# First attention of a two-layer block: the row scale takes the mask flag as an operand per partition, and moves with the mask maximum behind a second value copy

## The reference

```python
def _L0_xattn_ref(hidden_states, memory_tokens, memory_mask):   # hidden = layernorm(x), tokens (4, 1601, 256)
    scale = 1.0 / jnp.sqrt(jnp.asarray(D, hidden_states.dtype))
    scores = jnp.einsum('bsd,bmd->bsm', hidden_states, memory_tokens) * scale
    scores = jnp.where(memory_mask[:, None, :], scores, neg_inf)
    attn = jax.nn.softmax(scores, axis=-1)
    readout = jnp.einsum('bsm,bmd->bsd', attn, memory_tokens)
    valid_b = jnp.any(memory_mask, axis=-1)
    out = jnp.where(valid_b[:, None, None], readout, jnp.zeros_like(readout))
    return out
...
x = x + _L0_xattn_ref(_layernorm(x, axis=-1), ctx_2048, mask_BxS2_bk0)
```

## Time and profile before

| | |
|---|---|
| median of 3 runs | 760.24 us (758.79 to 761.08) |
| the profiled execution's own time | 762.05 us |
| its span in the profile | 759.1 us |
| busy over the span: PE / DVE / ACT / POOL | 92% / 72% / 52% / 23% |
| mean granted clock of PE | 0.97 of full speed |
| chain that ended last: PE / ACT / DVE / DMA | 64% / 11% / 10% / 3% |
| in it, `valid` L1571 and `rscale` L1626 | 1% each |

### The profile page before, as it was taken

How to read it: one execution, slowest core, us unless ns; L and a number is a source line. 1 busy time by engine, 2 the same in 40 slices (tenths; PEclk the granted TensorE clock), 3 DMA queues, 4 the chain that set the end, 5 groups by cost and what they waited for, 6 DMA issues and landing times.

```text
span 759.1 us, 14907 instructions
## 1 busy us (share of the span) xinstructions
PE 695.1 (92%) x5499; PEld 538.5 (71%) x5499; DVE 544.3 (72%) x1174; ACT 397.7 (52%) x564; POOL 173.8 (23%) x220
## 2 busy tenths in 40 slices
PE   3798999989889999999999699999999999998990
PEld 3798999988678888888888554454454454677880
DVE  6767576777486666666666788789888878766655
ACT  2643333334322322222222699999999999533550
POOL 5462524340000000000000050002303604442551
PEclk9899999999999999999999899999999999799996
DMA  7456484832627777677768959986969740464545
GB/s 247 133 172 227 134 293 146 266 125 89 201 65 242 231 255 239 209 224 243 253 217 170 149 81 168 189 128 95 221 92 201 119 67 2 151 253 130 165 129 190
DMA packets 55211, 131.14 MB, mean 173 GB/s; under 512 B 10112, under 2 KB 36096, under 8 KB 51568
## 3 DMA queue, kind: packets, MB, share of 16 engines
q1 hardware_dynamic: 51888, 122.93, 60.8%
q0 software_dynamic: 2256, 6.18, 2.4%
q10 hardware_dynamic: 1008, 1.25, 0.5%
HBM read 78.78 MB, written 48.79 MB: 168 GB/s over the span
## 4 chain that ended last, share of the span: by engine, by line
PE 64%; issue 11%; ACT 11%; DVE 10%; DMA 3%; SPq 1%; POOL 0%; DVEq 0%; POOLq 0%; ACTq 0%
PE ps L657 15%; PE ps L658 14%; PE ps L659 14%; ACT p L1439 8%; PE ps L1001 5%; PE ps L1189 4%; PE ps L959 3%; PE ps L1205 2%; PE ps L1023 1%; PE ps L741 1%; DVE valid L1571 1%; DVE rscale L1626 1%; PE ps L1173 1%; DMA raw<-in_ctxT 1%; ACT hh L1344 1%
## 5 line engine op out<-in xcount | busy, mean ns | idle before, releaser
L1439 ACT ACTIVATE p<-ps,kbias 128x1024 f32<-128x1024 f32 (+1 forms) x208 | 211.4, 1163 | 5.1 <-PE ps L959 4.9
L1950 DVE TENSOR_SCALAR p<-p 128x1024 f32<-128x1024 f32 (+1 forms) x208 | 140.8, 689 | 25.8 <-ACT p L1439 24.1
L1001 PE MATMUL ps<-p,vsl 128*17 128x256 f32 (+1 forms) x1664 | 114.2, 383 | 2.0 <-DVE p L1950 1.0
L959 PEld LDWEIGHTS ps<-qst,kst 48*128 48x128 f32 (+1 forms) x832 | 58.6, 182 | 60.0 <-ACT p L1439 32.1
L1344 ACT ACTIVATE hh<-h 128x512 fp32r<-128x512 f32 x50 | 31.6, 632 | 132.2 <-DVE h L1817 115.2
L959 PE MATMUL ps<-qst,kst 48*128 48x256 f32 (+1 forms) x832 | 91.1, 318 | 5.3 <-ACT p L1439 1.5
L360 POOL TENSOR_SCALAR nv<-mv 128x2 f32<-128x2 f32 x8 | 6.2, 777 | 358.8 <-DVE mv L1880 211.2
L657 PE MATMUL ps<-xTh,w_hi 128*128 128x512 f32 x200 | 79.8, 399 | 1.5 <-DVE h L1813 0.8
L658 PE MATMUL ps<-xTl,w_hi 128*128 128x512 f32 x200 | 79.2, 396 | 0.0
L659 PE MATMUL ps<-xTh,w_lo 128*128 128x512 f32 x200 | 78.9, 394 | 0.0
L1001 PEld LDWEIGHTS ps<-p,vsl 128*17 128x17 f32 (+1 forms) x1664 | 35.7, 96 | 40.0 <-DVE p L1950 7.2
(11 more groups left out here) (308 smaller groups left out, 1558.8 us busy)
## 6 DMA issues: line engine op xcount, KB each, us to landing
x_slots<-blank SPq DMA_DIRECT2D x20, 1032.0 KB, 5.9
kst<-k_hi SPq DMA_DIRECT2D x64, 200.2 KB, 8.4
w_raw<-in_w SPq DMA_DIRECT2D x25, 384.0 KB, 3.5
v_one<-vst SPq DMA_DIRECT2D x4, 1768.0 KB, 9.9
vsl<-v_one SPq DMA_DIRECT2D x4, 1768.0 KB, 17.0
kst<-k_lo SPq DMA_DIRECT2D x32, 200.2 KB, 8.5
raw<-in_ctxN SPq DMA_DIRECT2D x12, 512.0 KB, 5.6
e_w<-in_w SPq DMA_DIRECT2D x2, 3072.0 KB, 15.3
```

What stands on the lines that cost most here:

```text
L959: mm = pe.matmul(ps[0:rows, 2 * (x % RING) + t, c * SEQ:(c + 1) * SEQ], kst[r, job % KSL, c, m * P:m * P + rows], qst[r, b, 2 * g + c, :], ...
L1001: mm = pe.matmul(ps[32 * j:32 * j + VW, 6 + job % 2, 0:SEQ], vsl[0:rows, b % 2, at_:at_ + VW], p32[0:rows, x % PBUF, (2 * t + c) * SEQ:(2 ...
L1439: act.activation(p32[0:rows, x % PBUF, :], psf[0:rows, bank * 512:bank * 512 + 1024], ACT.Exp, scale=0.25, bias=kbias[0:rows, col:col + 1] ...
L1950: dve.tensor_scalar(t, t, CLO, CHI, ALU.max, ALU.min).then_inc(p_clip, 1)
```

## The change

`row_scale` multiplies `rsum` by `valid` with `tensor_scalar`, where `valid` is a scalar operand, one value per partition, in place of `tensor_tensor`, where it is a second input tensor of one column. And the two calls, `any_key(b)` (even steps) and `row_scale(i)` (every step), leave their place behind `add_readout` and stand behind the second `vev` of the step, ahead of the third. PE, ACT and SP have the same instructions in the same order as before, and so has POOL.

```diff
                 dve.wait_ge(rscale_rdy, 2 * i + 1)
-                dve.tensor_tensor(rscale[:], rsum[:], valid[:], ALU.mult).then_inc(rscale_rdy, 1)
+                dve.tensor_scalar(rscale[:], rsum[:], valid[:, 0:1], None, ALU.mult).then_inc(rscale_rdy, 1)
...
                 klo(b, h + 1)
                 if i:
                     add_readout(i - 1)
-                if h == 0:
-                    any_key(b)
-                row_scale(i)
                 if last:
                     next_stat(3, NT - 2)
                     next_mean(0, NT - 2)
...
                 vev(b, h)
                 ptl(i, 3)
-                for n in range(h + 1, h + 4):
+                vev(b, h + 1)
+                if h == 0:
+                    any_key(b)
+                row_scale(i)
+                for n in range(h + 2, h + 4):
                     vev(b, n)
                 if h == 0 and b + 1 < NB:
                     norm_lo(b + 1)
```

## The result

The changed kernel takes 753.23 us, the median of 4 runs (752.06 to 754.35), beside 760.66 us before (4 runs): a ratio of 0.990, 95% interval 0.987 to 0.993. In a second set it took 752.46 beside 761.30 us, again 0.990 (0.987 to 0.992). The forecast was 751.8, in 748.3 to 756.8: faster, by 8.4 us; measured are 7.4 and 8.8 us. The profiled execution went from 762.05 to 752.55 us, its span from 759.1 to 749.9.

What follows compares the result with a forecast made beforehand. PE, busy nearly all the time, was taken as the bound, with only its idle time to win. Steps 0, 2, 4 gave 6.0, step 6 2.1, step 7 0.3: 8.4 us off 760.24, so 751.8 us, range 748.3 to 756.8.

Steps and rivals of the forecast that it cites:

- The stall and its parts: Front of even steps: PE waits 9.1 us for `pTl`, behind `valid` 1.81, `rsum` 0.16, `rscale` 2.00 us, held by POOL.
- What the removal is worth: Even steps: 3.97 us leave the path to the first `pTl`; 2.0 us gained each in steps 0, 2 and 4.
- the load chain: End of even steps: context load, ACT's copies, `xTl`, then `sS`; issue 1.6 us sooner plus 0.4 for less queued.
- Step 6: No `norm_lo` and no next batch there, so it gets PE's own 2.07 us, summed as 2.1.
- The new place: Behind the second `vst`: 2.2 us of moved work hidden in 2.9 us of DVE idle time; cost 0.
- What would show it: Right: `rscale` 0.15 to 0.21 us, `pTl` wait under 1, load issued 1.6 us sooner, `sS` up to 1 us.
- a sign of being wrong: `rscale` row near 2 us, PE waiting over 1.5 us for `sS` or `vst` in each even step, or more slow-clock stretches.
- The sign for the clock: Wrong if the first 200 us show more slow-clock stretches than the two of steps 0 and 4.
- Step 7: 0.3 us (0.16 + 0.16) leave the front for a place where DVE waits for PE: 0.3 us gained.
- The rule: Trainium skill: `tensor_scalar` can take both port pairs and be held by POOL, making the new form no better there.
- rival (b): Half given back: new `rscale` or both calls held some 2 us by POOL's `cNl`, `sS` 1.3 us late; 757.0 us; chance 0.12.

Runs made afterwards that it cites:

- the move alone: Both calls moved to the new place but with the old two-input form, against the kernel before: 752.00 us, ratio 0.988.
- the doubled maximum: The whole change with the mask maximum taken twice in a row at the new place, against the kernel before: 757.57 us, ratio 0.994.
- the form alone: The row scale's new form (an operand per partition) at its old place, against the kernel before: 754.29 us, ratio 0.990.

## Why the prediction was right, point by point

**The stall and its parts: right.** `pTl` fell from 9.1 us to nothing, and 1.8 us put back in its place cost all the gain. That `rscale` ended with POOL's instruction is shown from both sides: 0.16 us for the same form where POOL is idle, 0.21 us for the other form inside POOL's work. One premise was too narrow: that only PE's idle time can be won. Of the 7.8 us in the even steps 2.7 are busy time, most of it slow clock behind the stalls of steps 0 and 4.

**What the removal is worth: right in step 2 but for 0.4 us, in steps 0 and 4 partly by luck.** In step 2 the end was the load chain: 1.6 us for the sooner issue, plus 0.4 for a shorter queue. Measured are 1.59 us and nothing (4.24 us against 4.22), and the step gave 1.56. Steps 0 and 4 were booked at the same 2.0, as having the same chain. After the change they have it: `sS` waits of 0.9 and 1.5 us, and the move alone, whose step 0 ran at a granted clock of 1.00 with PE 1.2 us less busy than after the whole change, was no shorter there (26.16 us). But before the change PE itself was last there, at its slow clock: there was no `sS` wait behind them, and in step 0 ACT's `xTh` waited 0.46 us for PE's transposes. That they gave 1.84 and 2.14, near 2.0, rests on where PE stood at that clock. In step 4 the load was issued 1.57 us sooner after the addition (7.62 to 6.05) and landed in 4.18 us for 4.64; so the landing was 0.46 shorter there and the same in step 2, and no run shows the 0.4 us as the price of the queue. Step 6, booked at 2.1, gave 2.28. In all 7.8 against 8.1.

**The new place: right.** 0.21 us as taken; 2.2 us hidden in steps 2 and 4. In the two steps that I did not work out, 0 and 6, there was less room: nothing was left behind the moved work, as the doubled maximum showed with 1.7 us each. In step 6 it just fits, since PE does not wait there. In step 0 it does not. ACT's `xTh` is ready at 37.14 + 0.58 = 37.72 (ACT in time, after):

```profile
37.14 0.58 ACT L1250 ACTIVATE xTh<-ps 128x512 fp32r<-128x512 f32 x1
```

but DVE comes to it at 38.20, without idle time:

```profile
38.20 0.68 DVE L1561 TENSOR_TENSOR xTl<-ps,xTh 128x512 fp32r<-128x512 f32 x1
```

So 0.5 of PE's 0.9 us for `sS` in step 1 is the price of the new place, booked at 0. The longer first `xn` of step 0 was not booked either; the move alone has it too (1.13 us), the form alone hardly (0.48 us).

**What would show it: `sS` up to 1 us was too low.** It is 1.5 in steps 3 and 5, at the edge of the 1.5 us named as a sign of being wrong, though not in each even step. The prediction's own numbers say more than 1 once the queue gives nothing: 2.84 for PE alone, less 1.6, is 1.24. Measured from the readout's addition, PE comes 1.58 us sooner to the third chunk in step 3 (82.86 - 67.88 = 14.98 to 80.41 - 67.01 = 13.40), and would have come 1.48 sooner still. The sign for the clock came out right: of the slow stretches of steps 0 and 4 the first is left, shorter, and the second is gone.

**Step 7: 0.3 was booked;** the rows give 0 to 0.2 (15.24 for the old place at full clock, with the new form; 15.06 and 15.21 for the new place), and the 1.8 us of the first profile belong to the clock.

**The rule: it held, but not for one column.** The Trainium skill, VectorE: DVE Perf Modes, section "Mode 2×_2P — use both read ports for one tensor", splits one source in two halves and so takes both port pairs. One column did not behave so in any of the seven starts inside POOL's subtractions with the form alone. The wider ones did: `xn`, 256 columns with two operands per partition, was held, 1.14 us for 0.40; and the mask's 1602 columns took 0.98 us, where the maximum over the same row takes 1.81, and twice made POOL's `cTl` 1.04 us longer. I gave rival (b) 0.12 for want of such a row, and the form alone settles it for one column.

## What to carry to other kernels

Before valuing an edit that takes work off a path, find the second latest input at the place where the path leaves the engine, and where the same step waits last: two edits here, which removed 1.8 and 3.9 us from the same front, were worth the same 7 to 9 us alone and together by the medians, since other inputs then held the step. When a wait goes and another takes its place, look whether one input feeds both that wait and the next: moving the wait alone gained nothing, bringing the load sooner about 2 us, the two together about 4. And a DVE form with two inputs in SBUF, even of one column, ended with POOL's instruction (up to 2.00 us for 0.16), where an operand per partition over one column did not (0.21 us). That is for one column: over 256 columns that form was held too.

## What the runs showed of the hardware that I had not expected

A `tensor_scalar` over 1602 columns, begun 0.2 us behind a POOL subtraction, made that longer by about its own length (2.25 us for 1.21, in two of two such starts), though POOL had begun first. Begun 0.9 us behind, it was itself 0.19 us longer. One over 256 columns, begun late in POOL's work, took 1.14 us for 0.40, while one over one column passed beside POOL in 0.21 us. An operand per partition costs 0.05 us over the two-input form on one column (0.21 against 0.16); the timings of the two forms at the new place can't be told apart. What decides between DVE and POOL is not shown. And stretches of the same 60 matmuls took 6.7 or 8.5 us in different executions (granted clock 1.00 or 0.80), 1.8 us, a fifth of the gain that a single profile shows: lengths of stretches have to be compared at one clock.
